# Attention values projected once for all groups, their bias added to the outputs, key parts taken from PSUM

## What is computed

```
xq = (inputs_q @ wq + bq).reshape(B, S, 16, 128)
xk = (inputs_q @ wk + bk).reshape(B, S, 4, 128)
xv = (inputs_q @ wv + bv).reshape(B, S, 4, 128)
qg = (xq * scale).reshape(B, S, 4, 4, 128)
attn = softmax(einsum('bqhgd,bkhd->bhgqk', qg, xk))
out = einsum('bhgqk,bkhd->bqhgd', attn, xv).reshape(B, S, 2048)
return out @ wo + bo
```

## Time and profile before

| | us |
|---|---|
| median of 3 runs | 1148.87 (1148.14 to 1150.42) |
| span of the profiled execution, first to last instruction | 1142.5 |
| what lies around that span, by the median | 6.4 |
| PE busy, share of the span | 1058.0, 93% |
| attention, up to the barrier behind it | about 623 |
| the last group's `v`, 48 matmuls of 128 columns | 5.4 |

### The profile page before, as it was taken

How to read it: one execution, slowest core, us unless ns; L and a number is a source line. 1 busy time by engine, 2 the same in 40 slices (tenths; PEclk the granted TensorE clock), 3 DMA queues, 4 the chain that set the end, 5 groups by cost and what they waited for, 6 DMA issues and landing times. The chain is left out here.

```text
span 1142.5 us, 18205 instructions
## 1 busy us (share of the span) xinstructions
PE 1058.0 (93%) x6276; PEld 891.7 (78%) x6276; DVE 758.7 (66%) x1312; ACT 599.1 (52%) x1027; POOL 561.4 (49%) x408
## 2 busy tenths in 40 slices
PE   5899999999999999999998899997977988999992
PEld 4788888888888888888886776654765787999992
DVE  4877764787556775667775644466788655777777
ACT  3566653666536665446662423433532255777772
POOL 1664622756236563355540347762314776544453
PEclk9999999999999999999999999998998989999996
DMA  7700240002400762000000146641200457666666
GB/s 196 52 28 1 58 36 3 19 11 38 56 2 24 207 218 69 1 1 1 1 2 24 58 137 212 215 136 56 106 2 6 161 191 240 207 221 219 225 212 199
DMA packets 45642, 109.94 MB, mean 96 GB/s; under 512 B 8519, under 2 KB 26069, under 8 KB 43504
## 3 DMA queue, kind: packets, MB, share of 16 engines
q1 hardware_dynamic: 38640, 95.46, 30.2%
q0 software_dynamic: 6912, 13.30, 3.1%
HBM read 94.27 MB, written 41.29 MB: 119 GB/s over the span
## 5 line engine op out<-in xcount | busy, mean ns | idle before, releaser
L422 POOL TENSOR_TENSOR at_prob<-at_prob,at_inv_sum 128x1024 f32<-128x1024 f32 x128 | 243.6, 1905 | 287.9 <-DVE at_inv_sum L647 287.9
L612 ACT ACTIVATE at_pt_h<-ps 128x512 fp32r<-128x512 f32 x256 | 139.1, 596 | 148.7 <-PE ps L537 148.6
L697 DVE TENSOR_TENSOR at_pt_l<-ps,at_pt_h 128x512 fp32r<-128x512 f32 x256 | 164.6, 685 | 60.8 <-ACT at_pt_h L612 60.7
L686 DVE TENSOR_REDUCE at_neg_max<-ps 128x1 f32<-128x1024 f32 x128 | 156.1, 1220 | 42.1 <-PE ps L41 41.7
L579 ACT ACTIVATE at_prob<-ps,at_neg_max 128x1024 f32<-128x1024 f32 x128 | 143.7, 1123 | 18.1 <-DVE at_neg_max L686 18.1
L537 PE MATMUL ps<-ident,at_prob 128*128 128x128 f32 x1024 | 133.8, 274 | 3.8 <-POOL at_prob L422 3.8
L2072 POOL DMA_INDIRECT lines<-f_y,f_x_raw x96 | 95.8, 998 | 82.7 <-ACT f_y L1990 54.7
L537 PEld LDWEIGHTS ps<-ident,at_prob 128*128 128x128 f32 x1024 | 120.0, 141 | 20.9 <-POOL at_prob L422 4.7
L39 PE MATMUL ps<-at_k_h,at_q_h 128*128 128x512 f32 x256 | 108.8, 425 | 0.0
L41 PE MATMUL ps<-at_k_h,at_q_l 128*128 128x512 f32 x256 | 100.7, 393 | 0.0
L39 PE MATMUL ps<-at_pt_h,at_v_h 128*128 128x512 f32 x256 | 100.5, 393 | 0.0
(11 more groups left out here) (308 smaller groups left out, 2541.7 us busy)
## 6 DMA issues: line engine op xcount, KB each, us to landing
e_raw<-in_we SPq DMA_DIRECT2D x32, 624.0 KB, 4.2
f_cw_row<-cw SPq DMA_DIRECT2D x32, 512.0 KB, 4.7
slots<-in_empty SPq DMA_DIRECT2D x4, 3456.0 KB, 46.3
f_x_raw<-slots SPq DMA_DIRECT2D x32, 432.0 KB, 4.8
lines<-in_empty SPq DMA_DIRECT2D x3, 2048.0 KB, 33.8
f_e_raw<-in_we SPq DMA_DIRECT2D x32, 128.0 KB, 2.8
at_wq_raw<-in_wq SPq DMA_DIRECT2D x4, 512.0 KB, 3.5
at_wo_raw<-in_wo SPq DMA_DIRECT2D x4, 512.0 KB, 3.3
```

The lines of the kernel that those rows point to most:

```text
L422: nc.gpsimd.tensor_tensor(prob[:, t % RING, :], prob[:, t % RING, :], inv_sum[:, t:t + 1].broadcast_to([P, T]), ALU.mult).then_inc(normed, 1)
L612: nc.scalar.activation(pt_h[:, e[1] % PT, :], turned(e[1]), ACT.Copy).then_inc(pt_high, 1)
L686: nc.vector.tensor_reduce(neg_max[:, t:t + 1], slot(n, start), AX.XY, ALU.max, negate=True).then_inc(maxed, 1)
L697: nc.vector.tensor_tensor(pt_l[:, e[1] % PT, :], turned(e[1]), pt_h[:, e[1] % PT, :].bitcast(F32), ALU.subtract).then_inc(pt_split, 1)
```

## The change

The values of all four groups are projected once, in the opening: a token tile is the stationary operand and all 512 value columns move, 6 matmuls of 512 columns for a tile, two tiles in an event, four events `v`. Two stand where `v` stood, and two behind the 12 leading `s`. ACT copies each from PSUM to `v_all`. The `v` of `change` goes. `wv` is loaded at once (512 KB) to the last piece of the ring of probabilities, and its two parts lie in `o_h`. The bias is kept per partition, `bv_now` takes the group's column at `vs`, and the ACT and DVE operations that split the outputs add it. `k` is split without `proj`: ACT writes the high part from PSUM and DVE the low part, which also frees the slot. The last half of `y` is cut in two events of two tiles. DVE waits for one more semaphore (`o_split`) at `vs`.

```diff
-    opening = [("k",), ("q", 0), ("v",)] + [("s", s) for s in range(LEAD)] + [("vs",)] + pair("t", 0)
+    outputs = [("y", j) for j in range(YS)]
+    opening = [("k",), ("q", 0)] + [("v", j) for j in range(VALUES // 2)] + [("s", s) for s in range(LEAD)]
+    opening += [("v", j) for j in range(VALUES // 2, VALUES)] + [("vs",)] + pair("t", 0)
...
-    change = [("k",)] + pair("p", at) + pair("t", at + 4) + [("v",)] + pair("p", at + 2) + pair("t", at + 6)
+    change = [("k",)] + pair("p", at) + pair("t", at + 4) + pair("p", at + 2) + pair("t", at + 6)
...
-    change += [("vs",)] + pair("s", 10) + [("y", 0)] + pair("t", 0) + [("y", 1)]
+    change += [("vs",)] + pair("s", 10) + outputs[:1] + pair("t", 0) + outputs[1:]
...
-                load(0, "kv", "q")
+                load(0, "k", "q")
+                sp.dma_start(wv_raw, net.dram["wv"]).then_inc(consts, 16)
...
-                sp.dma_start(bv[:, :], net.dram["bv"].partition_broadcast(P)).then_inc(consts, 16)
+                sp.dma_start(bv[:, :], net.dram["bv"]).then_inc(consts, 16)
...
+                pool.wait_ge(w_high, 2 + DC)
+                nc.gpsimd.tensor_tensor(wv_l, wv_raw, wv_h.bitcast(F32), ALU.subtract).then_inc(kv_split, 1)
...
                         if e[0] == "v":
-                            for i in range(TT):
+                            pe.wait_ge(kv_split, 2)
+                            for i in (2 * e[1], 2 * e[1] + 1):
                                 toks = slice(i * P, (i + 1) * P)
                                 for c in range(DC):
-                                    last = product(nc, slot(n, start)[:, i // 4, (i % 4) * P:(i % 4 + 1) * P], xn_h[:, c, toks],
-                                                   xn_l[:, c, toks], wkv_h[:, 1, c, :], wkv_l[:, 1, c, :], c == 0, c == DC - 1)
+                                    last = product(nc, slot(n, start)[:, i % 2, :], xn_h[:, c, toks], xn_l[:, c, toks],
+                                                   wv_h[:, c, :], wv_l[:, c, :], c == 0, c == DC - 1)
...
                             if e[0] == "k":
-                                ins = nc.scalar.activation(halves(proj[:, :]), slot(n, start), ACT.Identity,
-                                                           bias=bk[:, bass.ds(g + 1, 1)])
+                                nc.scalar.activation(halves(k_h[:, :]), slot(n, start), ACT.Identity,
+                                                     bias=bk[:, bass.ds(g + 1, 1)]).then_inc(proj_high, 1)
...
+                        if e[0] == "v":
+                            exps()
+                            act.wait_ge(values_full, e[1] + 1)
+                            nc.scalar.activation(v_all[:, 2 * e[1]:2 * e[1] + 2, :], slot(n, start), ACT.Copy).then_inc(v_read, 1)
...
+                act.wait_ge(consts, 80)
+                nc.scalar.activation(wv_h, wv_raw, ACT.Copy).then_inc(w_high, 1)
...
                         if e[0] == "vs":
                             inverts(0 if start == 0 else 3)
                             if start:
                                 dve.wait_ge(pv_done, LIFT + STEPS * (g + 1))
-                            dve.wait_ge(v_added, own + 1)
-                            nc.vector.tensor_copy(v_h[:, :], v_full[:, :]).then_inc(v_high, 1)
+                                dve.wait_ge(o_split, LIFT + UNITS * (g + 1))
+                            dve.wait_ge(v_read, VALUES)
+                            tiles = lambda ap: ap.rearrange("p (i d) -> p i d", d=DH)
+                            values = v_all[:, :, bass.ds(own * DH, DH)]
+                            nc.vector.tensor_copy(bv_now[:, :], bv[:, bass.ds(own, 1)])
+                            nc.vector.tensor_copy(tiles(v_h[:, :]), values).then_inc(v_high, 1)
```

More of the change, by code:

```diff
@@ L268, in softmax_attention_phase @@
         closing += pair("p", n) + (pair("t", n + 4) if n + 4 < STEPS else [])
-    closing += [("y", 0), ("y", 1)]
+    closing += outputs
     def jobs_of(events):
@@ L385, in _ @@
                     sp.dma_start(wo_raw[:, :, :], net.dram["wo"][g]).then_inc(wo_loaded, 16)
-                    sp.wait_ge(wkv_split, g + 1)
-                    load(g + 1, "kv")
+                    sp.wait_ge(kv_split, g + 2)
+                    load(g + 1, "k")
                     sp.wait_ge(wq_split, 2 * (g + 1))
@@ L501, in run @@
                             if e[0] == "k":
-                                pe.wait_ge(wkv_split, g + 2)
+                                pe.wait_ge(kv_split, g + 3 if start else 1)
                             elif start == 0 or e[1] == PER:
@@ L532, in run @@
                             u, kt = divmod(e[1], KT)
+                            if start == 0:
+                                pe.wait_ge(v_read, VALUES - 1)
                             if kt == 0:
@@ L553, in run @@
                                 pe.wait_ge(o_split, LIFT + UNITS * (g + 1))
-                            for i in range(TT // 2):
-                                toks = slice((e[1] * TT // 2 + i) * P, (e[1] * TT // 2 + i + 1) * P)
+                            for k, i in enumerate(Y_TILES[e[1]]):
+                                toks = slice(i * P, (i + 1) * P)
                                 for hh in range(PER):
-                                    last = product(nc, tokens_of(slot(n, start), i), o_h[:, hh, toks], o_l[:, hh, toks],
+                                    last = product(nc, tokens_of(slot(n, start), k), o_h[:, hh, toks], o_l[:, hh, toks],
                                                    wo_h[:, hh, :], wo_l[:, hh, :], hh == 0, hh == PER - 1)
@@ L650, in lows @@
                         while later:
-                            e = later.pop(0)
+                            e, job = later.pop(0)
                             dve.wait_ge(proj_high, proj_count(g, e))
-                            hi, lo = (k_h[:, :], k_l[:, :]) if e[0] == "k" else (q_h[:, e[1] % 2, :], q_l[:, e[1] % 2, :])
-                            nc.vector.tensor_tensor(lo, proj[:, :], hi.bitcast(F32), ALU.subtract).then_inc(proj_split, 1)
+                            if e[0] == "k":
+                                nc.vector.scalar_tensor_tensor(halves(k_l[:, :]), slot(job, start), bk[:, bass.ds(g + 1, 1)],
+                                                               halves(k_h[:, :]).bitcast(F32), ALU.add, ALU.subtract).then_inc(proj_split, 1)
+                            else:
+                                nc.vector.tensor_tensor(q_l[:, e[1] % 2, :], proj[:, :], q_h[:, e[1] % 2, :].bitcast(F32),
+                                                        ALU.subtract).then_inc(proj_split, 1)
                     for place, e in enumerate(events):
@@ L660, in run @@
                         if e[0] in "kq":
[L661 removed]
+                            later.append((e, n))
                             if start == 0:
                                 lows()
[L664 to L671 removed]
                         if e[0] == "vs":
```

116 lines of the change are left out of this document (57 added, 59 removed).

## The result

| | kernel before | changed kernel |
|---|---|---|
| median, us | 1148.73 (4 runs, 1148.14 to 1150.42) | 1135.96 (4 runs, 1135.03 to 1137.68) |
| ratio | | 0.9882 [0.9869, 0.9895] |
| profiled execution: span, us | 1142.5 | 1135.8 (its own time 1137.68) |
| first transposes of attention, us | 39.40 | 43.13 |
| attention's end (VectorE's `n_root` behind the barrier), us | 623.41 | 608.04 |

The change made the kernel 13.6 us faster by the ratio (12.8 us by the two medians), where 16.2 us were forecast. The time of 1135.96 lies in the range and 3.3 us over the forecast. Attention ended 15.4 us sooner; the part behind it, which the change does not touch, took 8.7 us longer in this one trace.

What follows compares the result with a forecast made beforehand. Attention was taken to run at PE's pace. Laps -16.1 + 0.45, opening +0.8 and end -1.3 sum to -16.15 us, from 1148.87 to 1132.7 us; range 1130.0 to 1137.5.

Steps and rivals of the forecast that it cites:

- The laps: Three changes of group: without `v`, 5.36 us less each, -16.1 us, plus 0.45 us for stalls.
- The stall of the transposed pieces: Change of group: transposes 56 and 57 wait for DVE's splits, about 0.1 to 0.2 us; 0.15 taken a lap.
- The cover: Chains `v` had hidden in each lap: probabilities 2.3 us to spare, new keys 1.6, transposed pieces about 0.
- The opening: Before attention's first transposes: more `v`, less idle time, clock held; +0.8 us, with ends at 0.5 and 2.5.
- the split of the values: DVE in the opening: 1.36 and about 1.3 us, in time for PE; at 2.80 us it would be 1.5 late.
- The end: Last read of `y` and moments cover two tiles instead of four, so the barrier comes 1.3 us earlier: -1.3.
- The loop's head: PE's waits at the two jumps back, 3.7 us, left as they are; up to 3.7 would go if `y`'s read caused them.
- What lies around the span: Time outside the profiled span of 1142.5 us: 6.4 us, said to stay.
- Missed cover: Rival: one of the laps' three chains is later, PE stops 1.5 to 3 us a lap; 1138.7 us at 2; chance 0.09.
- costly opening: Rival: the opening takes the projection almost whole, +5 instead of +0.8 us, 1136.9 us; chance 0.07.
- late constants: Slower rival at the start: values' weights ready after `v` is due; 5 us to spare; 10 more give 1159; chance 0.04.
- pace by columns: Rival: matmul time goes by columns, 128 costing 0.059 us; laps -8.4, opening +3.4, 1143 us; chance 0.01.

Runs made afterwards that it cites:

- before_again: The kernel before, no edit, run and traced a second time; ratio 1.0003 [0.9986, 1.0019] to the kernel before.
- all_ahead: Changed kernel with all four value jobs ahead of the leading scores instead of two ahead and two behind; ratio to the kernel before 0.9922 [0.9897, 0.9947].
- pe_unrolled: Changed kernel with TensorE's three laps written out, other engines keeping their hardware loop; ratio to the kernel before 0.983 [0.9796, 0.9863].
- after_look: The changed kernel, no edit, traced once more in a single run; 1131.50 us, 0.984 of the kernel before's median on that chip.
- start_filled: Changed kernel with two calls of fill matmuls on TensorE between the opening's transposes and the key projection; ratio to the kernel before 0.988 [0.9846, 0.9914].
- k_old: Changed kernel with the keys' old path (ACT to proj, ACT to high part, DVE from proj); ratio to the kernel before 0.9926 [0.9909, 0.9942], 1134.1 us.
- narrow: Changed kernel with its value projection in matmuls of 128 columns instead of 512; ratio to the kernel before 0.9999 [0.9972, 1.0026].
- y_two: Changed kernel with the last group's output projection in two events of four tiles instead of 4, 2 and 2; ratio to the kernel before 0.9879 [0.9859, 0.9899].
- before_both: Kernel before with TensorE's laps written out and its idle time ahead of the keys filled; ratio to the kernel before 0.999 [0.9971, 1.0009].

## Why the prediction was right and where it was off

**Direction and size.** Faster, in the range, 3.3 us from the forecast (1132.7 for 1135.96). By the ratios of the two comparisons, 13.6 and 15.1 us (of 1148.73 and 1144.05), against 16.15. The ends of the range are not the sums that the forecast names for them: these give 1130.4 and 1136.8, where 1130.0 and 1137.5 stand.

**The laps** held: -16.1 + 0.45 forecast. With the idle time at the loop heads taken off and full clock in the lap, from the first `y` to the next, it is 148.0 us before (before_again, 149.48 less 1.46) and 142.5 after (144.38 less 1.89): 5.5 us, of which 5.26 lie between first key matmul and first `y` (5.21 forecast); the other 0.25 lie ahead of the keys and are in no term. The stall of the transposed pieces was 0.05 instead of 0.15 us a lap, and without the new path of the keys it is 1.03: the edit on the keys earns its place as said.

**The cover** held on all three chains; the probabilities have 2.34 us to spare (2.3 forecast), the keys 1.66 (1.6).

**The opening**, +0.8 forecast. Its parts are right: 24 matmuls at 0.233 us in place of 3.5 us of idle time (all_ahead brings 3.68 back), no slow stretch behind the transposes, the split of the values 0.91 + 1.23 us (1.36 + 1.3 forecast). Three traces of either kernel show the stretch from the first transposes to the first `y` 6.9 us shorter (137.7 to 137.9, and 130.8), 5.4 of it `v`, and 1.5 the stretch at 1.2 GHz behind the old idle time, forecast as 0.8 + 0.6. The step that failed is one that the forecast did not take: it left the keys ahead of all this at 2.4 GHz without a word, since they ran so in the one trace. In all three traces of the changed kernel they ran at 1.2 GHz for a while, in one of three of the kernel before: about 1.2 us more than forecast, on average over these.

**The end**: 1.24 us for 1.3.

**The loop's head** was left at 3.7 us, rightly, and the jump named as its cause, rightly (pe_unrolled). Missed was that it costs a second time behind it. Stretches at 1.2 GHz followed 3 of 6 loop heads in the changed kernel's three traces, 1 of 6 in the kernel before: 1 us on average. It is not a property of the changed kernel, since in after_look, start_filled and all_ahead none followed.

**Sum for attention**: over three traces of each kernel it ends at 622.6 and 607.5 us on average, 15.1 sooner. Forecast 16.15; with the measured parts -17.2 (opening +2.1, first part of lap 1 -6.9, two laps -11.0, the rest -1.4), of which the clock at the start gives back 1.2 and the clock at the loop heads 1.0. Behind attention the three traces give 521.0 and 523.5 us, 2.5 more, within the 518 to 528 over which the traces of the kernels and their variants scatter. That the whole came out within 3.3 us of the forecast rests in part on this scatter; the terms of attention are what the traces bear out.

**What lies around the span** was wrong by its size: 6.4 us, as the difference of a median and one span. The changed kernel's profiled execution lies 1.9 us over its span, and so do the others (1.8 to 2.2). So the profiled execution of the kernel before was near 1142.5 + 1.9 = 1144.4 us, some 4 us faster than the median of its runs; this is worked out from the other traces, its own time is not known. It did no harm to a difference that was taken off the median.

**The rivals.** Missed cover, costly opening, late constants and pace by columns all did not come; the first and the last were tried (k_old, narrow), the opening's two bounds by all_ahead. Late constants need no run: the last constant (`at_bo`) landed at 13.89 us in the changed kernel's first trace, 13.52 before, the values' weights were split at 18.91 us (19.5 forecast) and the first `v` came at 23.77 without a wait. Nothing waits at the first `v` in any trace.

**What stays open**: whether the changed kernel's keys meet 1.2 GHz more often than those of the kernel before (8 of 8 traces with the idle time left in, 4 of them with a clock that had not risen yet, against 1 of 3), what makes the idle times put down to issue behind attention, and whether the jump waits for its code, as the packets beside it suggest.

## What to carry to other kernels

Project a shared operand once, at the full 512 columns, and put part of it where the engine would stand idle anyway; then follow every chain that the removed work had hidden, since one of them (here the split of the keys) costs over 1 us a lap if left as it was. Count an idle time of TensorE of about 2 us with what may follow it at 1.2 GHz, here 1.5 us more in about half of the cases, and look at more than one trace before calling a stretch's clock a property of the kernel. A hardware loop's jump is idle time as well: with three laps in the loop, writing TensorE's out was worth 4.1 to 7.5 us in attention of the changed kernel, and, together with the fill, no more than 1.6 in the one trace of the kernel before, which had a stop elsewhere.

## What the runs showed of the chip that was not expected

- TensorE's jump back to the head of its loop: 1.40 to 2.02 us of idle time in 22 loop heads, 0 written out. It ended 1.61 to 1.83 us behind the end of a 16 KB packet on the queue of instructions, each time.
- Idle times of 1.72 to 2.02 us at loop heads were followed by a stretch at 1.2 GHz in 9 of 17 cases, those of 1.40 to 1.65 us in none of 5; but the 1.56 us in narrow, amid its matmuls of 128 columns, was. Behind the 2.01 us ahead of the keys the clock fell in 5 of 11 traces, was still down in 4 and stayed up in 2; it fell in none of 3 where fill matmuls took the place. The stretch usually costs 1.55 us (eight matmuls of 512 columns at 0.427 instead of 0.234 us), 2.5 to 2.7 at the start of k_old and y_two, 3.3 behind the stop in before_both and 4.9 behind the one in narrow.
- The same idle time of 3.5 us ahead of the first transposes was followed by 1.2 GHz in the kernel before in three traces, and by 2.4 GHz in before_both and in all_ahead (3.68 us).
- A matmul of 128 columns takes 0.111 us at 2.4 and 0.213 at 1.2 GHz, one of 512 columns 0.234 and 0.427.
